# Second layer of a graph attention kernel: late source scores from a folded W2, target and shift rows through DRAM

## The reference

```python
def gat(x, W, a_src, a_dst, bias, concat):
    h = (x @ W).reshape(N, H, C)
    al_s = einsum('nhc,hc->nh', h, a_src)         # source score
    al_d = einsum('nhc,hc->nh', h, a_dst)         # target score
    e = leaky_relu(al_s[src] + al_d[dst], 0.2)
    ex = exp(e - segment_max(e, dst)[dst])
    alpha = ex / (segment_sum(ex, dst)[dst] + 1e-16)
    out = segment_sum(h[src] * alpha, dst)
    return (out if concat else out.mean(heads)) + bias
hid = elu(gat(x, W1, ...))       # 768 -> 4 heads of 512, so hid is 1250 x 2048
out = gat(hid, W2, ...)          # 2048 -> one head of 768
result = layernorm(x + out)
```

## Time and profile before

| | |
|---|---|
| median of 3 runs | 938.28 us (937.78 to 938.47) |
| profiled execution: time, span | 937.02 us, 935.1 us |
| PE matmul busy | 881.1 us, 94% |
| PE weight load busy | 796.9 us, 85% |
| DVE busy | 602.1 us, 64% |
| ACT busy | 424.4 us, 45% |
| POOL busy | 198.1 us, 21% |
| mean granted TensorE clock | 0.987 |
| chain that ended last, by engine | PE 67%, DVE 11%, issue 9%, POOL 6%, ACT 3%, DMA 2% |

### The profile page before, as it was taken

How to read it: one execution, slowest core, us unless ns; L and a number is a source line. 1 busy time by engine, 2 the same in 40 slices (tenths; PEclk the granted TensorE clock), 3 DMA queues, 4 the chain that set the end, 5 groups by cost and what they waited for, 6 DMA issues and landing times.

```text
span 935.1 us, 15156 instructions
## 1 busy us (share of the span) xinstructions
PE 881.1 (94%) x5719; PEld 796.9 (85%) x5719; DVE 602.1 (64%) x1169; ACT 424.4 (45%) x686; POOL 198.1 (21%) x134
## 2 busy tenths in 40 slices
PE   4998879999999999999999999989999999699996
PEld 2455557799888998889988899989999999599996
DVE  9458663668873889638895488672223334497886
ACT  5456452276643866339652396661111111487300
POOL 1000000144212332124321244300000000155452
PEclk9999989999999999999999999999999999799999
DMA  8609999462548237472174243655223322400223
GB/s 298 145 14 132 178 174 159 135 211 81 177 138 239 67 103 212 112 231 78 29 214 139 68 142 117 174 166 115 72 48 70 85 48 30 102 1 2 69 84 95
DMA packets 64450, 111.18 MB, mean 119 GB/s; under 512 B 31772, under 2 KB 33464, under 8 KB 63004
## 3 DMA queue, kind: packets, MB, share of 16 engines
q1 hardware_dynamic: 64379, 110.22, 45.7%
HBM read 85.25 MB, written 24.94 MB: 118 GB/s over the span
## 4 chain that ended last, share of the span: by engine, by line
PE 67%; DVE 11%; issue 9%; POOL 6%; ACT 3%; DMA 2%; DVEq 1%; SPq 1%; POOLq 0%; ACTq 0%
PE ps L1726 19%; PE ps L1728 19%; PE ps L1727 19%; POOL pbuf L608 5%; PE ps L1755 3%; PE ps L1696 2%; PE ps L1847 2%; PE ps L1686 1%; DVE pbuf L621 1%; DVE h2f L1632 1%; DMA mask_scratch<-nbs 1%; DVE h2f L1606 1%; DVE vbuf L1440 1%; DMA w1f<-in_L_gnn_W 1%; DVE bnst L1623 1%
## 5 line engine op out<-in xcount | busy, mean ns | idle before, releaser
L608 POOL TENSOR_TENSOR pbuf<-pbuf,grow 125x625 f32<-125x625 f32 x100 | 169.9, 1700 | 701.2 <-ACT pbuf L593 261.1
L1726 PE MATMUL ps<-hx,PThi 125*125 125x260 f32 (+5 forms) x800 | 227.3, 284 | 3.0 <-DVE vbuf L1441 2.5
L1728 PE MATMUL ps<-hx,PTlo 125*125 125x260 f32 (+5 forms) x800 | 225.4, 282 | 0.0
L1727 PE MATMUL ps<-hlo,PThi 125*125 125x260 f32 (+4 forms) x800 | 224.9, 281 | 0.0
L1726 PEld LDWEIGHTS ps<-hx,PThi 125*125 125x125 f32 x800 | 148.7, 186 | 7.0 <-DVE vbuf L1441 2.9
L1727 PEld LDWEIGHTS ps<-hlo,PThi 125*125 125x125 f32 x800 | 149.1, 186 | 1.4
L1728 PEld LDWEIGHTS ps<-hx,PTlo 125*125 125x125 f32 x800 | 149.0, 186 | 0.0
L1726 PE MATMUL ps<-W2p,hT 128*125 128x384 f32 x320 | 109.7, 343 | 3.2 <-DVE hT L1453 1.7
L1728 PE MATMUL ps<-W2p,hT 128*125 128x384 f32 x320 | 108.1, 338 | 0.0
L1727 PE MATMUL ps<-W2p,hT 128*125 128x384 f32 x320 | 108.1, 338 | 0.0
L621 DVE SCALAR_TENSOR_TENSOR pbuf<-pbuf,counts 125x625 f32<-125x625 f32 x100 | 90.7, 907 | 25.3 <-ACT pbuf L615 25.2
(11 more groups left out here) (186 smaller groups left out, 1571.6 us busy)
## 6 DMA issues: line engine op xcount, KB each, us to landing
xr<-xT_scratch SPq DMA_DIRECT2D x30, 750.0 KB, 4.9
nbm<-mask_scratch SPq DMA_DIRECT2D x40, 273.4 KB
hidden_scratch<-vbuf SPq DMA_DIRECT2D x40, 224.0 KB
hblk<-hidden_scratch SPq DMA_DIRECT2D x10, 896.0 KB
xT_scratch<-xa SPq DMA_DIRECT2D x20, 375.0 KB, 11.7
w1f<-in_L_gnn_W SPq DMA_DIRECT2D x12, 512.0 KB, 9.1
w1raw<-in_L_gnn_W SPq DMA_DIRECT2D x4, 1536.0 KB, 7.9
w2raw<-in_L_gnn_W SPq DMA_DIRECT2D x14, 384.0 KB, 5.4
```

The source lines that it names most:

```text
L608: pool.tensor_tensor(pslot(c), pslot(c), src[:, g * GN:(g + 1) * GN], ALU.add).then_inc(e_done, 1)
L1726: pe.matmul(dst, ahi, bhi, start=start, stop=False, skip_group_check=shared)
L1727: pe.matmul(dst[:, 0:n], ahi, blo, start=False, stop=False, skip_group_check=shared)
L1728: return pe.matmul(dst, alo, bhi, start=False, stop=stop, skip_group_check=shared)
```

## The change

It has three parts.

1. *Fold.* While heads 0 to 2 run, DVE multiplies each of W2's 16 blocks of 128 rows by the second layer's source vector and sums over the columns: 16 numbers per partition, `w2a`, five in each of the first two heads and six in the third, at chunks `b` = 0, 1, 5, 8, 9 (and 7) of the second half. SP loads each block of W2 into the single buffer `wf2` after the fold before it is done. The result is stored to DRAM.
2. *Late source scores.* Blocks 8 and 9's source scores are dot products of their hidden features (in `hblk`) with the folded vector, loaded in three parts into `prow`: `late_dots`. They are then known before those blocks' products. Scores of blocks 7, 8 and 9 go through DRAM as one store and one load; the maxima of the third and fourth parts and the first half of the shift are done in DVE's turn of block 8, before or right after that turn's `split_hT`. Since `nbp2` and `prow` lie in `h2f`'s last two blocks, ACT evicts block 8 only when all maxima are done.
3. *Rows.* Target and shift rows go as columns to DRAM and come back spread, in two halves, with waits on SP; PE's spreads and ACT's copies of them are gone. The last block's eviction, its target score and the second half's shift move behind the first chunk's steps.

```diff
+FOLD2 = tuple((h, b) for h in range(H - 1) for b in ((0, 1, 5, 8, 9) if h < H - 2 else (0, 1, 5, 7, 8, 9)))
@@ SP
+            def load_fold2(h, b):
+                if (h, b) in FOLD2:
+                    i = FOLD2.index((h, b))
+                    if i > 0:
+                        sp.wait_ge(fold2_done, i)
+                    sp.dma_start(wf2[:], W2[128 * i:128 * i + 128, :]).then_inc(ld_fold2, 16)
+
             for h in range(H - 1):
...
+                load_fold2(h, 0)
                 if h > 0:
                     for t in range(GT):
                         store_hid(NB * h - GT + t)
                 load_drow(h + 1, 0)
+                load_fold2(h, 1)
                 if h + 2 < H:
...
                         load_nb(h + 1, b)
+                    load_fold2(h, (5, None, 7, None, 8)[t])
                 store_shift(h + 1)
                 load_grow(h + 1, 0)
                 load_xr(h + 1, NB - 2)
+                load_fold2(h, 9)
...
+            def load_prow(p):
+                lo_c, hi_c = PP[p]
+                if p > 0:
+                    sp.wait_ge(dot_done, 2 * p)
+                else:
+                    sp.wait_ge(w2a_stored, RS)
+                for lo, hi in RP:
+                    sp.dma_start(prow[lo:hi, 0:hi_c - lo_c], spread_row(w2a_d.rearrange("k p -> (k p)")[lo_c:hi_c], hi - lo)).then_inc(ld_a2, 16)
@@ SP, after block 6's scores
+            load_prow(1)
+            load_prow(2)
+            sp.wait_ge(ht_ps, 2 * NB - 2)
+            load_part(1)
+            sp.wait_ge(al2_done, 2 * NB - 4)
+            sp.wait_ge(s2_late, 1)
+            store_s2(NB - 3, NB)
+            load_part(2)
+            sp.wait_ge(s2_stored, RS * (NB - 2))
+            load_s2(NB - 3, NB, ld_s2[QP])
+            sp.wait_ge(g_stored, RS * H)
+            load_row(drow2, d2_d, 0, ld_drow[0])
+            sp.wait_ge(g_done, H + 1)
+            store_column(g2_d, gcol[:, H * NB:H * NB + GT], 0)
+            sp.wait_ge(g_stored, RS * (H + 1))
+            load_row(grow2, g2_d, 0, ld_grow[0])
@@ ACT, loop over blocks
+                if b == NB - 2:
+                    act.wait_ge(mx_last, QP * NB)
+                if b < NB - 1:
+                    h2_out(b)
@@ ACT, first chunks
             act_exp(act, CHUNKS)
+            act_hi(act, CHUNKS)
+            act_exp(act, CHUNKS + 1)
+            h2_out(NB - 1)
+            act.wait_ge(h2_sb, NB)
@@ DVE, heads
+                if g == 1 and (h, b) in FOLD2:
+                    i = FOLD2.index((h, b))
+                    dve.wait_ge(ld_fold2, RS + 16 * (i + 1))
+                    dve.wait_ge(fold2_done, i)
+                    dve.scalar_tensor_tensor(wf2junk[:], wf2[:], 1.0, as2row[:], ALU.mult, ALU.mult, accum_out=w2a[:, i:i + 1]).then_inc(fold2_done, 1)
@@ DVE, layer two
+            for b in range(NB - 1):
+                if b > 0:
                     split_hT(2 * b + 2)
...
                 if b == 7:
                     maxima2(8)
                     maxima2(9)
+                    late_dots(1)
                     for m in range(4):
                         part_maxima2(0, m)
                 if b == 8:
+                    for m in range(NB):
+                        part_maxima2(1, m)
+                    merge(1)
+                    for m in range(6):
+                        part_maxima2(2, m)
+                split_hT(2 * b + 3)
+                if b == 8:
+                    for m in range(6, NB):
+                        part_maxima2(2, m)
+                    merge(2)
+                    shift2(0)
+                scores2(b)
+                if b == 6:
+                    late_dots(0)
+                if b == 7:
+                    late_dots(2)
+                    late_scores()
                     for m in range(4, NB):
                         part_maxima2(0, m)
                     merge(0)
...
+            split_h2(0)
+            dve_counts(dve, CHUNKS)
+            dve_lo(dve, CHUNKS)
+            scores2(NB - 1)
+            shift2(1)
@@ PE, between products and chunks
-            pe.wait_ge(al2_done, 2 * NB - 1)
-            spread(lambda n: al2[:, 0, n:n + 1], lambda b: (7, 0), NB - 1, NB).then_inc(bc2_ps, 1)
-            pe.wait_ge(al2_done, 2 * NB)
-            spread(lambda n: al2[:, 1, n:n + 1], four_from(0)).then_inc(bc2_ps, 1)
-            pe.wait_ge(g_done, H + 1)
-            for g in range(2):
-                spread(lambda n: gcol[:, H * NB + n:H * NB + n + 1], lambda n: (4 + n // GT * 2 + n % GT // BB, n % GT % BB * B),
-                       g * GT, (g + 1) * GT).then_inc(bc2_ps, 1)
             pe.wait_ge(h2x_one, 1)
-            pe.wait_ge(g2_sb, 2)
```

More of the change, by code:

```diff
@@ L573, in pslot @@
         def pslot(c):
[L575 removed]
+            return pbuf[:, c % PR, :] if c < CHUNKS else pbuf2[:, (c - CHUNKS) % PR, :]
         def hi_slot(c):
@@ L590, in act_relu @@
             src, bias = (drow, s_up[:, h, b:b + 1]) if h < H else (drow2, s2_up[:, b:b + 1])
-            if h < H and b == 0:
+            if b == 0:
                 act.wait_ge(ld_drow[g], RS * (h + 1))
@@ L810, in _ @@
                 load_grow(h + 1, 1)
+            sp.wait_ge(fold2_done, KC)
+            for lo, hi in ((0, XP), (XP, 128)):
+                sp.dma_start(w2a_d.rearrange("k p -> p k")[lo:hi, :], w2a[lo:hi, :], allow_slow_non_contiguous=True).then_inc(w2a_stored, 16)
             sp.wait_ge(mk_done, H * NB)
@@ L1553, in merge, with late_dots, late_scores, shift2 @@
                 dve.tensor_tensor(mx[:, lo:hi], mx[:, lo:hi], mxp[:, p * NB:(p + 1) * NB], ALU.max).then_inc(mx_all, 1)
-            for b in range(NB):
-                if b > 0 and b + 1 < NB:
+            dots = bnst[:, 0:2, 0, 0:len(PP)]
+            def late_dots(p):
+                lo, hi = PP[p]
+                dve.wait_ge(ld_a2, 2 * RS + RS * (p + 1))
+                dve.wait_ge(al2_done, 2 * NB - 6 if p < 2 else 2 * NB - 4)
+                for b in (NB - 2, NB - 1):
+                    if p > 0 or b == NB - 1:
+                        dve.wait_ge(dot_done, 2 * p + b - NB + 2)
+                    if p == 0:
+                        dve.wait_ge(ld_hb[b % 2], RS * (b // 2 + 1))
+                    dve.scalar_tensor_tensor(a2junk[:, 0, 0:hi - lo], hblk[:, b % 2, lo:hi], 1.0, prow[:, 0:hi - lo], ALU.mult, ALU.mult,
+                                             accum_out=dots[:, b - NB + 2, p:p + 1]).then_inc(dot_done, 1)
+            def late_scores():
+                dve.wait_ge(dot_done, 2 * len(PP))
+                dve.tensor_reduce(al2[:, 0, NB - 2:NB], dots, AX.X, ALU.add).then_inc(s2_late, 1)
+            def shift2(g):
+                lo, hi = H * NB + g * GT, H * NB + (g + 1) * GT
+                dcol = al2[:, 1, g * GT:(g + 1) * GT]
+                dve.wait_ge(mx_all, QP)
+                dve.wait_ge(al2_done, (2 * GT, 2 * NB - 2)[g])
+                dve.scalar_tensor_tensor(mneg[:, lo:hi], mx[:, lo:hi], -1.0, dcol, ALU.mult, ALU.subtract).then_inc(m_neg, 1)
+                dve.wait_ge(m_neg, H + 1 + g)
+                dve.scalar_tensor_tensor(negm[:, lo:hi], mneg[:, lo:hi], SLOPE, mneg[:, lo:hi], ALU.mult, ALU.min).then_inc(m_sb, 1)
+                dve.wait_ge(m_sb, H + 1 + g)
+                dve.scalar_tensor_tensor(gcol[:, lo:hi], negm[:, lo:hi], 1 / SLOPE, dcol, ALU.mult, ALU.add).then_inc(g_done, 1)
+            for b in range(NB - 1):
+                if b > 0:
                     split_hT(2 * b + 2)
@@ L1569, in _ @@
                     merge(0)
-                if b + 1 < NB:
-                    split_hT(2 * b + 3)
-                if b == NB - 1:
-                    for m in range(NB):
-                        part_maxima2(1, m)
-                    merge(1)
-                scores2(b)
             def split_h2(b):
@@ L1581, in split_h2 @@
                 dve.tensor_tensor(h2lo[:, b, :], h2f[:, b, :], h2x[:, b, 0:D].bitcast(F32), ALU.subtract).then_inc(h2_lo, 1)
-            for b in range(NB):
-                part_maxima2(2, b)
-            merge(2)
-            dve_shift(dve, H, al2[:, 1, :])
+            split_h2(0)
[3 more added lines that the diff above has]
+            shift2(1)
             def evict2(n):
@@ L1948, in _ @@
                 for u, order in enumerate(ORDER2):
+                    if c == 0 and u < 2:
+                        pe.wait_ge(h2_sb, NB - 1 + u)
                     for t, i, first in order:
```

133 lines of the change are left out of this document (69 added, 64 removed).

## The result

The changed kernel takes 942.78 us (median of 6 runs, 941.05 to 944.59), the kernel before 938.33 (6 runs, 937.78 to 938.66) on the same chip: ratio 1.0052, 95% interval 1.0036 to 1.0069, 4.5 us slower. On two more chips the ratio was 1.0078 (1.0059 to 1.0097) and 1.0082 (1.0061 to 1.0103). The forecast was 936.9, with no more than 940.0 in its range. The profiled execution took 942.59 us, its span 940.8: 5.7 more than the span of before.

The account below looks back on a forecast made before the run. Between 810.5 and 873.1 the POOL, ACT, DVE chunk loop sets the end, so P, its first POOL add, matters. -2.9 (earlier P) + 1.5 (given back) = -1.4 us: most likely 936.9, range 934.3 to 940.0.

Parts of the forecast that it names:

- The folds: Heads: 16 DVE multiplies, 15.2 us, hidden from PE; tightest at chunk b = 1, margin 0.7 us, price 0.
- Last scores complete at 771.3: Layer two: folded vector's parts loaded behind SP's read at 757.31, then DVE's dots; s2 complete at 771.3, PE not held.
- the second half's late stores: Chunk loop: second half's rows leave about 815, are there by 830, used after 840; price 0.
- Store 8.0, row 4.2: Scores of blocks 7 to 9 over DRAM: store 8.0 us, row load 4.2, so DVE's second-part maxima can start at 783.5.
- DVE's list 11.5: DVE's maxima, merges, shift steps and one hT split from 783.5 to the finished shift: 11.5 us, ending at 795.0.
- Trip of the shift 12.6: Shift row's store, completion and load through DRAM instead of PE's spreads: 12.6 us, ends 10.9 and 15.2.
- the P of 807.6: Start of layer two's first POOL add: 807.6 against 810.51 before, 2.9 us earlier.
- the 1.26 that I had added: From profiled execution to median: the runs' median of before, 938.28, lay 1.26 us above that execution's time.
- PE stall 2.0 in the last block, free: Last block: hT split ends at 792.4, PE wants it at 790.4; 2.0 us stall, costing nothing at the end.
- Give-back 1.5: Loop behind P: h2's last eviction, last target score and shift steps return 1.5 of the 2.9 us; ends 0.8 and 2.5.
- PE's clock: PE's restart after 12 us idle: low clock again, perhaps longer than 3.0 us; hidden by PE's spare 2.0, grown to 3.5.
- B: Two store completions between 771 and 804: every microsecond beyond 16.0 costs; 940.9 us with both at 10.0; chance 0.12.

Follow-up runs that it names:

- e3: The kernel before with only the sixteen folds added, the folded vector neither stored nor used: 938.34 us, ratio 0.9991 to the kernel before.
- e14: The changed kernel with the target's column store moved behind the row load of the last scores: 942.44 us, ratio 1.0038 to the kernel before.
- e15: The changed kernel with the target's first five scores stored as 125 runs of 20 bytes instead of 625 4-byte pieces: 941.62 us, ratio 1.0035 to before.
- e10: The changed kernel with the target's column store issued twice, the second into scratch: 952.26 us, ratio 1.0148 to the kernel before.
- e6: The changed kernel, DVE splitting the last half of hT ahead of the second and third parts' maxima: 941.35 us, ratio 1.0032 to before.
- e4: The changed kernel with chunk 2's relu ahead of h2's last eviction, chunk 1's counts ahead of the last score and shift steps: 942.14 us, ratio 1.0040.
- e7: The changed kernel with target store late, third mask part behind score row, last split ahead of maxima, last eviction, score and shift before first exp: 935.06 us.
- e13: The changed kernel unaltered, timed again as reference on the third chip: 946.38 us, ratio 1.0082 to the kernel before.
- e11: The changed kernel with the target's column store issued from ACT's queue, still ahead of hblk 9 and block 6's score: 947.49 us, ratio 1.0096 to before.

## Why the prediction was wrong

*The folds* (margin 0.7, price 0): right, e3 shows it. In the changed kernel DVE waited for W2's rows 7.4 us in five places, and PE did not.

*Last scores complete at 771.3*: wrong, and the step that decided. It took SP's read of block 6's scores at 757.31 from the trace of before; it came at 762.05, 0.8 of it the offset at the start of layer two and 3.9 the longer store. The middle part of the folded vector then took 5.7 us to DVE's dot (762.84 to 768.53) instead of 4.9. So the scores were complete at 776.9 instead of 772.1, 4.8 late. The step had counted the loads in SP's queue and the wait for the folded parts, but had no term for the target's column store between block 5's and block 6's score; only the second half's late stores had been looked at, at 0. Moving it gave back 3.9 us of kernel (e14), cutting its pieces 4.8 (e15); doubling it cost 6.7 (e10).

*Store 8.0, row 4.2*: the store took 7.4, the row 6.2. The term of the row was short by 1.9, since the mask's third part is issued between the two; without it the row took 4.6.

*DVE's list 11.5*: 11.4. *Trip of the shift 12.6*: 11.7 (801.90 to 813.62). Both sizes hold, and with them the statement that a trip costs some 9 us more than PE's spreads. Taken together: 0.8 + 4.8 - 0.6 + 1.9 - 0.1 - 0.9 = 5.9 us of the 6.0 between the P of 807.6 that I gave and 813.62. With the give-back below, the span missed by 7.1 us (933.7 and 940.8). The median missed by only 5.9, since it lay 0.2 above the profiled execution and not the 1.26 that I had added; that is luck.

*PE stall 2.0 in the last block, free*: it was 7.9, since the row came later, and free all the same (e6).

*Give-back 1.5*: 2.3 to 2.5, the upper bound; DVE's first shift step took 1.14 us beside a POOL add, 0.17 where it stood alone. e4 shows that putting the pieces off recovers only 0.5, e7 that ahead of the loop they cost nothing.

*PE's clock*: after the 8.8 us without matmuls the granted clock was 0.51 for 5.7 us from the restart (1.2 GHz of the two levels; 3.0 us in the earlier trace rows), as forecast without effect on the end, since PE still waits at the second restart.

```profile
818.90:824.60 5.70, 5.65 (x27) 5.68 (x28) 4.99 (x9) 3.85 (x6) 1.29 (x1) 0.51 0.17 5
```

*The rivals.* B had the right side (940.9) and the wrong place: the two completions it priced came to 7.4 + 6.7 = 14.1 us, under its 16.0. The loss sits in a store that no case named. The rows gave no price for it: SP's wait is 7.5 us in the mean behind columns of 125 pieces and 6.9 behind columns of 1250, so a column's own completion says nothing of what its pieces do to a transfer asked for behind it, and the earlier trace rows have none with another transfer right behind it. The new store stood in SP's list of the changed kernel, though, and could have been named as a term of unknown size; the sum had it at nothing.

## What to carry to other kernels

A DMA that writes a column of single elements can cost twice: its own completion, and the time that its pieces hold up what is asked for behind it. List what is issued in the next 10 us. Here 625 pieces in SP's queue held up a store by 4 to 5 us on one chip and 6.5 on another, and another issuing queue did not help; longer runs, or a later place, did. Work that is put behind a serial loop's first step is still in the loop: here it was free only in the wait ahead of it.

## What the runs showed of the hardware that I had not expected

- 500 fewer 4-byte pieces in one store, same bytes and same queue, took 7.7 us off the store behind it in one profile each (16.8 to 9.1; the same kernel as e13 had 12.4 and 13.1 on other chips) and 4.8 us off the kernel, e13 against e15. Until the pieces were through, the DMA engines showed shares of 0.86 to 1.06 at 29 to 47 GB/s.
- Behind the same 625 pieces issued from ACT's queue at 739.44, loads that SP issued from 740.16 on reached DVE only from 754.92 on, with the DMA engines nearly idle (0.07) from 744 to 748, e11. By what, is open.
- Where both were first timed the changed kernel scattered more (3.5 us from fastest to slowest, against 0.9); on the first chip of the experiments the kernel before scattered by 8.2 us, and the changed kernel's ratio went from 1.0052 to 1.0082 by chip. Why is left open.
